# Expert weights as raw high operands, their low halves cut and subtracted on VectorE

## The reference

```
x = layernorm(x + attention(x, w_q, ..., gn_bias))
logits = x @ router_w.T
top_vals, top_idx = top_k(logits, 1)
scores = sigmoid(-inf everywhere, top_vals at top_idx)
xr = x[None] * scores.T[:, :, None]
gate, up = split(einsum('eth,ehf->etf', xr, gate_up_proj))
routed = einsum('etf,efh->eth', up * silu(gate), down_proj).sum(0)
shared = silu(x @ shared_gate_w) * (x @ shared_up_w) @ shared_down_w
x = layernorm(x + shared + routed)
```

## Time and profile before

| What | Value |
|---|---|
| Device time, three executions | 563.60, 563.06 and 563.30 us, median 563.30 us |
| Device time of the profiled execution | 563.31 us |
| Its span in the trace | 561.5 us (1.8 us lie around it) |
| TensorE (PE) busy | 544.7 us, 97% |
| VectorE (DVE) busy | 415.7 us, 74% |
| GpSimd (POOL) busy | 322.6 us, 57% |
| ScalarE (ACT) busy | 234.1 us, 42% |
| Granted TensorE clock, mean | 0.998 of full speed |

### The profile page before, as it was taken

How to read it: one execution, slowest core, us unless ns; L and a number is a source line. 1 busy time by engine, 2 the same in 40 slices (tenths; PEclk the granted TensorE clock), 3 DMA queues, 4 the chain that set the end, 5 groups by cost and what they waited for, 6 DMA issues and landing times.

```text
span 561.5 us, 11872 instructions
## 1 busy us (share of the span) xinstructions
PE 544.7 (97%) x3884; PEld 455.9 (81%) x3884; DVE 415.7 (74%) x866; ACT 234.1 (42%) x415; POOL 322.6 (57%) x320
## 2 busy tenths in 40 slices
PE   7998999999999999999999899999999999999994
PEld 6776788778779779779778678888888888888884
DVE  5898977878877877977966787747866666666664
ACT  3435442555453463363353766133333333333331
POOL 0535493496395396296294383716786556666644
PEclk9999999999999999999999999999999999999999
DMA  8901206306607507606375623666677665556651
GB/s 257 305 18 39 76 2 82 108 26 136 215 4 185 190 2 169 207 1 175 115 266 188 226 87 113 234 216 181 198 165 216 183 187 188 187 195 197 194 182 39
DMA packets 46506, 83.56 MB, mean 149 GB/s; under 512 B 11584, under 2 KB 30528, under 8 KB 46432
## 3 DMA queue, kind: packets, MB, share of 16 engines
q1 hardware_dynamic: 38736, 64.27, 36.9%
q0 software_dynamic: 6048, 15.39, 10.0%
q10 hardware_dynamic: 1664, 3.15, 1.5%
HBM read 60.85 MB, written 22.34 MB: 148 GB/s over the span
## 4 chain that ended last, share of the span: by engine, by line
PE 90%; DVE 3%; POOL 2%; issue 1%; ACT 1%; POOLq 0%; ACTq 0%; DVEq 0%
PE duo L1660 51%; PE duo L2039 9%; PE duo L1884 6%; PE duo L1716 5%; PE duo L1738 4%; PE duo L2049 3%; PE duo L1888 2%; PE duo L1874 1%; PE duo L1820 1%; PE duo L1928 1%; PE duo L1778 1%; PE duo L1864 1%; PE duo L1796 1%; DVE sims L1149 1%; DVE turned L1129 1%
## 5 line engine op out<-in xcount | busy, mean ns | idle before, releaser
L1660 PE MATMUL duo<-w_gu_hi,xsT 128*128 x320 | 107.7, 399 | 0.0
L1660 PE MATMUL duo<-x1T,wsgu 128*128 128x512 f32 x384 | 93.2, 395 | 0.0
L1660 PEld LDWEIGHTS duo<-x1T,wsgu 128*128 128x128 f32 x384 | 70.9, 188 | 15.6
L935 POOL TENSOR_TENSOR turned<-turned,swapped 128x1024 f32<-128x1024 f32 x16 | 38.5, 2424 | 65.2 <-DVE swapped L1140 65.2
L1076 POOL DMA_INDIRECT out_rows<-of,seat x39 | 39.4, 1012 | 56.0 <-DVE of L1617 53.8
L1660 PEld LDWEIGHTS duo<-w_gu_hi,xsT 128*128 128x128 f32 x320 | 59.7, 188 | 11.3
L1660 PE MATMUL duo<-w_gu,xsT 128*128 x160 | 61.5, 384 | 0.0
L1572 DVE SCALAR_TENSOR_TENSOR eh<-duo,seat,e_act 128x512 f32<-128x512 f32 x38 | 28.5, 751 | 40.1 <-PE duo L1660 34.2
L1149 DVE TENSOR_TENSOR sims<-duo,causal 128x512 f32<-128x512 f32 x64 | 41.2, 686 | 15.1 <-ACT sims L682 15.1
L1067 POOL DMA_INDIRECT xz<-xz_d,seat x39 | 44.9, 1152 | 9.2 <-issue 9.0
L682 ACT ACTIVATE sims<-duo 128x256 f32<-128x256 f32 x64 | 21.1, 382 | 68.6 <-PE duo L1716 68.2
(11 more groups left out here) (192 smaller groups left out, 1279.7 us busy)
## 6 DMA issues: line engine op xcount, KB each, us to landing
dn_rest<-dn_lo_d SPq DMA_DIRECT2D x39, 512.0 KB
w_gu<-L_ffn_gate_up_proj SPq DMA_DIRECT2D x8, 1024.0 KB, 7.5
x_in<-x_t SPq DMA_DIRECT2D x8, 512.0 KB
x_res<-L_attn_x SPq DMA_DIRECT2D x8, 512.0 KB, 4.3
xz_d<-zs SPq DMA_DIRECT2D x8, 512.0 KB, 6.5
dn_raw<-L_ffn_down_proj SPq DMA_DIRECT2D x8, 512.0 KB
dn_hi_d<-dn_top SPq DMA_DIRECT2D x8, 512.0 KB, 3.5
dn_lo_d<-dn_low SPq DMA_DIRECT2D x8, 512.0 KB
```

The costliest lines, as they stand in the source:

```text
L935: nc.gpsimd.tensor_tensor(turned[:, g, :, :], turned[:, g, :, :], swapped[:, g, :, :], ALU.add)\
L1660: last = mm(out_, left(a, k), right(b, k), start=start and k == 0 and n == 0, stop=stop and k == kt - 1 and n == len(PASSES) - 1)
```

## The change

The high operand of the experts' matmuls becomes the raw weight, read as float32r. `w_gu_hi`, the ScalarE passes `expert_hi` and `down_top`, and the stores and loads of `dn_hi_d` are gone; `w_dn` is loaded straight from the input. The low half is made in two instructions: an AND of the bit pattern with `TOP_BITS` (-4096, so the lowest 12 bits are cleared) into the buffer of the low half, and a subtraction of that from the raw weight in place. The ANDs, eight of 128 x 2048 (`expert_cut`) and eight of 128 x 1024 (`down_cut`), are on VectorE. The subtractions stay where they were, but expert 1 takes the place of expert 5 on GpSimd, and VectorE's are in steps 7 to 9.

```diff
+TOP_BITS = -4096
-        w_gu_hi = sb("w_gu_hi", [P, EXPERTS, KT, 2 * FF], F32R)
+        w_gu_lo = sb("w_gu_lo", [P, EXPERTS, KT, 2 * FF], F32R)
 # SyncE
-                sp.dma_start(dn_hi_d[rows, :], f32(dn_top[:, :])).then_inc(sig.dn_top_out, 16)
                 sp.dma_start(dn_lo_d[rows, :], f32(dn_low[:, :])).then_inc(sig.dn_low_out, 16)
             def down_in(e):
-                sp.dma_start(f32(w_dn[:, e, :, :]).rearrange("p f d -> p (f d)"), dn_hi_d[P * e:P * (e + 1), :])\
+                sp.dma_start(w_dn[:, e, :, :], down[e].rearrange("(k p) n -> p k n", p=P)).then_inc(sig.edn_in, 16)
 # ScalarE: expert_hi and down_top with all their calls are removed
-                nc.scalar.activation(w_gu_hi[:, e, :, :], w_gu[:, e, :, :], ACT.Copy).then_inc(sig.ew_hi, 1)
-                nc.scalar.activation(dn_top[:, :], dn_raw[:, :], ACT.Copy).then_inc(sig.dn_top_ok, 1)
 # GpSimd, ahead of the row gathers
-            pool.wait_ge(sig.plan_ok, 2)
-            expert_rest(5, EXPERTS - 1)
+            expert_rest(1, 3)
 # VectorE
+            def expert_cut(e):
+                dve.wait_ge(sig.egu_in[e], 16)
+                ...
+                nc.vector.tensor_scalar(w_gu_lo[:, e, :, :].bitcast(I32), w_gu[:, e, :, :].bitcast(I32), TOP_BITS, None,
+                                        ALU.bitwise_and).then_inc(sig.ew_cut, 1)
             def expert_lo(e, n):
-                dve.wait_ge(sig.ew_hi, n)
-                nc.vector.tensor_tensor(w_gu[:, e, :, :].bitcast(F32R), w_gu[:, e, :, :], f32(w_gu_hi[:, e, :, :]),
+                dve.wait_ge(sig.ew_cut, n)
+                nc.vector.tensor_tensor(w_gu_lo[:, e, :, :], w_gu[:, e, :, :], f32(w_gu_lo[:, e, :, :]),
                                         ALU.subtract).then_inc(sig.ew_lo, 1)
+            def down_cut(e):
+                dve.wait_ge(sig.dn_raw_in, 16 * (e + 1))
+                if e:
+                    dve.wait_ge(sig.dn_low_out, 16 * e)
+                nc.vector.tensor_scalar(dn_low[:, :].bitcast(I32), dn_raw[:, :].bitcast(I32), TOP_BITS, None,
+                                        ALU.bitwise_and).then_inc(sig.dn_cut_ok, 1)
             def last_products(f):
+                expert_lo(2, 4)
                 shared_product(f, 0)
                 shared_product(f, 1)
+                expert_cut(3)
                 expert_lo(3, 5)
-                for j in range(2, FT):
-                    shared_product(f, j)
-                expert_lo(4, 6)
-                expert_lo(7, 8)
+                shared_product(f, 2)
+                expert_cut(5)
+                expert_lo(5, 6)
+                shared_product(f, 3)
+                for e, n in ((4, 7), (7, 8)):
+                    expert_cut(e)
+                    expert_lo(e, n)
 # VectorE, in the loop over steps, between variance and x_lo
+                if t == PAIRS - 1:
+                    expert_cut(EXPERTS - 2)
+                if t in PARTED:
+                    down_cut(PARTED[t][0])
 # VectorE, between the two halves of shared_sum
+                    if t in PARTED and len(PARTED[t]) > 1:
+                        down_cut(PARTED[t][1])
```

More of the change, by code:

```diff
@@ L184, in build @@
         sb = tensors(ctx)
-        w_dn = sb("w_dn", [P, EXPERTS, FT, D], F32R)
+        w_dn = sb("w_dn", [P, EXPERTS, FT, D])
         w_gu = sb("w_gu", [P, EXPERTS, KT, 2 * FF])
-        w_gu_hi = sb("w_gu_hi", [P, EXPERTS, KT, 2 * FF], F32R)
+        w_gu_lo = sb("w_gu_lo", [P, EXPERTS, KT, 2 * FF], F32R)
         first = ExitStack()
@@ L371, in build @@
             dn_raw_in = new("dn_raw_in")
-            dn_top_ok = new("dn_top_ok")
+            dn_cut_ok = new("dn_cut_ok")
             dn_low_ok = new("dn_low_ok")
-            dn_top_out = new("dn_top_out")
             dn_low_out = new("dn_low_out")
@@ L377, in build @@
             ehT_low_ok = new("ehT_low_ok")
-            ew_hi = new("ew_hi")
+            ew_cut = new("ew_cut")
             ew_lo = new("ew_lo")
@@ L823, in _ @@
                         squared(a)
-                    if t == PAIRS:
-                        expert_hi(0)
                 if has(t):
@@ L829, in _ @@
                     logits_copy(f)
-                    if t == PAIRS:
-                        expert_hi(1)
-                    if t == PAIRS + 1:
-                        expert_hi(5)
-                        expert_hi(7)
                 if has(t + 1) and t != 1:
@@ L869, in _ @@
                         y_top(a)
-                    if t == 3:
-                        expert_hi(EXPERTS - 2)
-                    if t in PARTED and len(PARTED[t]) > 1:
-                        down_top(PARTED[t][1])
                     if t == 1:
@@ L882, in _ @@
             act.wait_ge(sig.gu_ps, 2 * FT * PAIRS)
-            act.wait_ge(sig.dn_top_out, 16 * EXPERTS)
             for e in range(4):
-                act.dma_start(f32(w_dn[:, e, :, :]).rearrange("p f d -> p (f d)"), dn_hi_d[P * e:P * (e + 1), :])\
-                    .then_inc(sig.edn_in, 16)
+                act.dma_start(w_dn[:, e, :, :], k_rows(down[e])).then_inc(sig.edn_in, 16)
             def rows_hi(s):
@@ L975, in expert_rest @@
             def expert_rest(e, n):
-                pool.wait_ge(sig.ew_hi, n)
-                nc.gpsimd.tensor_tensor(w_gu[:, e, :, :].bitcast(F32R), w_gu[:, e, :, :], f32(w_gu_hi[:, e, :, :]),
+                pool.wait_ge(sig.ew_cut, n)
+                nc.gpsimd.tensor_tensor(w_gu_lo[:, e, :, :], w_gu[:, e, :, :], f32(w_gu_lo[:, e, :, :]),
                                         ALU.subtract).then_inc(sig.ew_lo2, 1)
@@ L986, in down_rest @@
             def down_rest(e):
-                pool.wait_ge(sig.dn_top_ok, e + 1)
-                if e:
-                    pool.wait_ge(sig.dn_low_out, 16 * e)
-                nc.gpsimd.tensor_tensor(dn_low[:, :], dn_raw[:, :], f32(dn_top[:, :]), ALU.subtract)\
+                pool.wait_ge(sig.dn_cut_ok, e + 1)
+                nc.gpsimd.tensor_tensor(dn_low[:, :], dn_raw[:, :], f32(dn_low[:, :]), ALU.subtract)\
                     .then_inc(sig.dn_low_ok, 1)
@@ L1489, in _ @@
                 elif t == PAIRS:
+                    expert_cut(0)
                     x1_lo(f)
                     variance(a)
+                    dve.wait_ge(sig.eps_ok, PAIRS)
                     expert_lo(0, 2)
@@ L2010, in _ @@
                     output(a)
-            gu_flat = (w_gu_hi[:, :, :, :].rearrange("p e k n -> p (e k n)"),
-                       w_gu[:, :, :, :].rearrange("p e k n -> p (e k n)").bitcast(F32R))
+            gu_flat = (w_gu[:, :, :, :].rearrange("p e k n -> p (e k n)").bitcast(F32R),
+                       w_gu_lo[:, :, :, :].rearrange("p e k n -> p (e k n)"))
             halves = (ehT, ehT_lo)
-            dn_flat = w_dn[:, :, :, :].rearrange("p e f n -> p (e f n)")
+            dn_flat = w_dn[:, :, :, :].rearrange("p e f n -> p (e f n)").bitcast(F32R)
             def slot_gate_up(s, e):
```

47 lines of the change are left out of this document (15 added, 32 removed).

## The result

The changed kernel takes 573.74 us in the median of four runs (573.30 to 575.22), the kernel before beside it on the same chip 563.39 us. The ratio is 1.0187, 95% interval [1.0175, 1.0199], so the change costs 10.4 us. The profiled execution took 573.30 us (span 571.5), against 563.31 (span 561.5) before: +10.0 us. These are the 10.0 us that the traces account for.

The account below looks back on a forecast made before the run. TensorE was taken as busy without a gap nearly throughout, so added VectorE work costs only where it makes TensorE late; 4.6 + 1.3 = 5.9 us on 563.31 gave 569.2 us, 80% range 566.5 to 573.0.

Parts of the forecast that it names:

- The price of one AND: On VectorE, two elements per tick: 1.23 us for 128x2048 and 0.70 us for 128x1024.
- Steps 3 to 6, down weights, and step 7's AND: ANDs fit into VectorE's waits but delay GpSimd's `var_e`, so TensorE loses 0.25 us in each of five steps: +1.3 us.
- Step 7, expert 6's subtraction: The 2.20 us subtraction between `yT_lo` and `zs` is hidden by waits for TensorE: nothing, upper end 1.2 us.
- Step 9: VectorE's solid chain from 351.65, lengthened by four ANDs, starts slot 0's matmuls late: +4.6 us, upper end +8.8.
- Step 8, "I give it nothing": Removing ScalarE's `expert_hi` passes frees none of TensorE's 2.7 us idle time: nothing, at best the whole 2.7.
- The clock falls in the new gap: Rival: TensorE's 3.4 us idle before slot 0 halves the clock for its first matmuls: +2.8 us, 572.0 us; chance 0.06.
- DMA: 4 MB of stores go, and the raw `w_dn` load's shorter rows no longer wait before TensorE does: nothing.

Follow-up runs that it names:

- run 4: Changed kernel with the five ANDs directly behind the variance in steps 3 to 7 cut to 8 columns; 573.24 us.
- run 8: Changed kernel's whole arithmetic reordered: two memsets before expert 0's subtraction, several ANDs moved, TensorE's wait for low weights moved to slot 0's last four matmuls; 565.46 us.
- run 6: Kernel before with only the down weights' part of the change, the first AND of a step placed behind `x_lo`; 564.83 us.
- run 10: Kernel before with only the down weights' part, first AND behind `x_lo`, and expert 6's subtraction in step 7 instead of step 3; 564.20 us.
- run 9: Changed kernel's whole arithmetic without padding, ANDs moved into idle time, expert 0's subtraction behind the first product; 567.06 us.
- run 1: Changed kernel with two tiny dependent memsets on VectorE before expert 0's subtraction in step 8; 571.44 us.
- run 11: As run 9, but expert 0's subtraction ahead of the first product behind two memsets, and expert 7's AND ahead of `zs`; 564.09 us.
- run 5: Kernel before with only the down weights' part of the change, its eight 128x1024 ANDs where the change puts them; 566.16 us.
- run 7: Changed kernel with two memsets before expert 0's subtraction, and step 9's four ANDs and the five behind the variance cut to 8 columns; 564.31 us.
- run 3: Changed kernel with the four ANDs of step 9 (experts 3, 5, 4 and 7) cut to 8 columns; 568.15 us.

## Why the prediction was wrong

The side was right and the time was not: 573.74 us against 569.2, above the range's end of 573.0.

- **The price of one AND: right.** 1.22 and 0.69 us measured, 1.23 and 0.70 forecast.
- **Steps 3 to 6, down weights, and step 7's AND: the mechanism right, the size partly by luck.** 1.3 us forecast, 1.23 measured. Runs 4 and 8 give it back by shortening or by moving the AND, each to within 0.1 us. But the working had `hT_lo` 0.5 us late and a slack of 0.26. In step 4 it is 0.38 us late, because `var_e` grew by 0.37. And of the 0.26 only 0.10 is slack, because TensorE starts 0.16 us behind the end of `hT_lo` (169.30 to 169.46). The two errors cancel. In step 7 `var_e` grew by 0.90 us and TensorE lost only 0.22 (its matmuls on `hT_hi` start at 299.05, 1.33 us later than before, of which 1.11 were lost earlier), so counting it like the others was luck as well. No wait on `hT_lo` has a line of its own; the loss shows only in the starts of the steps.
- **Step 7, expert 6's subtraction: right** at nothing (run 4: 308.71 against 308.65). Runs 6 and 10 show that this move was needed.
- **Step 9: mechanism right, size 0.5 us short.** 4.6 forecast, 5.12 measured. Of the four ANDs in the chain the first two took 1.45 and 1.35 us instead of 1.22, beside GpSimd's gathers (0.36 us). The other 0.2 us are the way from `xsT`'s end at 372.10 to the matmul at 372.36, for which the working had 0.04.
- **Step 8, "I give it nothing": this step failed**, by 2.09 us. Its argument looked at what ScalarE's passes hold back and found nothing that would be earlier. But a thing did become earlier, the subtraction, and that was the harm. The rows stood in the trace: the subtraction's wait of 1.01 us for `w_gu_hi`, and the power 0.54 us ahead of it. The Trainium skill (SBUF — State Buffer, section "SBUF: two separate sides"), which the prediction used for the AND, also counts a VectorE instruction with two SBUF inputs, against a GpSimd one that reads SBUF, among those that take the port pair, and says that whichever starts first keeps it for its whole length. The trace agrees where VectorE is first (+2.1 us, +2.0 in run 9). Where GpSimd is first it does not: before and in runs 1 and 11 the subtraction ran at 2.29 us in the middle of a power, and the measurement decides.
- **"The clock falls in the new gap": put into the sum at nothing, as a rival with a chance of 0.06, and it came. This is the second step that failed.** +1.49 us in the profiled execution instead of the rival's 2.8, and 2.4 in run 4. The 4.5 us after the last matmul were taken as proof that 3.4 us do no harm. In the changed kernel the clock was whole throughout a gap of 3.25 us too, and fell 0.6 us after work had begun: a clock read while the engine idles says nothing about the microseconds that follow. In run 4 it had fallen before work began again, behind a gap of 3.38 us.
- **DMA: right for this kernel** (no wait for `w_dn` in its trace). But runs 5 and 10 have one of 1.3 us and runs 6 to 9 and 11 none, so the raw load lies close to its need. What decides it was not tried.

The sum of the parts, 0.09 + 1.23 + 2.09 + 5.12 + 1.49 = 10.0 us, is the difference of the two profiled executions. Of the 4.5 us between 569.2 and 573.74, step 8 and the clock are 3.6, step 9 is 0.5, and the changed kernel's median lies 0.44 above its profiled execution.

## What to carry to other kernels

Where an engine's work is taken away, list which instructions elsewhere waited for it, and look at what they will now start beside: work that becomes earlier can cost as much as work that is added. Sum the gaps that a change opens ahead of dense matmuls, and put the clock's fall into the sum as a term with a range rather than as a rare rival. And before such a change is given up, try its order: here the same arithmetic cost 10.4 us in one order and at most 1 us in another.

## What the runs showed of the hardware

- A two-input subtraction of 128x2048 on VectorE that is running when GpSimd's power of 128x16 would start holds the power until it ends (2.1 us in step 8, 2.0 in run 9, from a lead of 0.05 and 0.15 us). A power that has started neither slows the subtraction nor is slowed by it (5.80 us for two before and in runs 1 and 11, where the subtraction was over before the second power, by the estimate in run 9).
- An AND of 128x2048 on VectorE takes 1.22 us; beside GpSimd's row gathers 1.35 to 1.45 us, and beside GpSimd's subtraction of 4.58 us in step 9 it took 2.06 us.
- The clock fell for gaps of 3.25 us and, in run 8, where 1.38 us and two shorter ones lay close together. It stayed whole in runs 5 and 10, where TensorE waited 1.32 and 1.28 us for `w_dn`, in run 3 with 0.68 us, in run 9 with 0.91 us and in run 11. So the length of the gap alone does not say whether it falls.
